# A 13-stage decoder on one core: TensorE multiplies constants into an unread bank behind the scores that run ahead

## The reference, cut to what matters

```
scores = q @ k.T (/ sqrt(8), + mask)          # 256 x 256
p      = softmax(scores, axis=-1)
out    = p @ v                                # 256 x 8
```

## Time and profile before

| | us |
|---|---|
| median of 3 timed runs | 1590.61 |
| profiled execution, own time | 1582.52 |
| its span (first to last instruction) | 1580.7 |
| TensorE busy | 1209.8 (77%) |
| TensorE weight loads | 607.2 (38%) |
| VectorE busy | 984.1 (62%) |
| ScalarE busy | 881.5 (56%) |
| GpSimd busy | 543.8 (34%) |

### The profile page before, as it was taken

One profiled execution on the slowest core, in us unless ns is written; L12 is line 12 of the kernel. 1 busy time (PEld: TensorE's weight loads), 2 busy tenths in 40 slices (PEclk: granted clock), 3 DMA queues, 4 the chain that ended last, 5 costly groups with the idle time before them and its releaser, 6 DMA issues. The chain is left out here.

```text
span 1580.7 us, 21176 instructions
## 1 busy us (share of the span) xinstructions
PE 1209.8 (77%) x6990; PEld 607.2 (38%) x6990; DVE 984.1 (62%) x1994; ACT 881.5 (56%) x1817; POOL 543.8 (34%) x673
## 2 busy tenths in 40 slices
PE   8999647266666677987657995977968988979886
PEld 3675422022222233542213552433444434734562
DVE  3673455999999927632757735446546658727752
ACT  3674144599999926874124871234634745724643
POOL 1462014488888843200224212011101223503440
PEclk9999887599999987998877997987986999999998
DMA  3000000000000015101006200015114110000000
GB/s 149 2 2 1 22 9 0 0 0 0 1 0 0 0 73 141 22 34 40 0 3 196 50 2 18 0 33 124 16 56 125 37 56 1 2 1 1 1 2 13
DMA packets 44108, 48.75 MB, mean 31 GB/s; under 512 B 3808, under 2 KB 40800, under 8 KB 42848
## 3 DMA queue, kind: packets, MB, share of 16 engines
q1 hardware_dynamic: 40688, 45.83, 10.0%
q10 hardware_dynamic: 3312, 1.57, 0.3%
HBM read 34.28 MB, written 13.11 MB: 30 GB/s over the span
## 5 line engine op out<-in xcount | busy, mean ns | idle before, releaser
L1548 POOL TENSOR_TENSOR L_attn_z<-L_attn_state,L_attn_r 128x1024 f32<-128x1024 f32 x64 | 151.0, 2360 | 21.6 <-DVE L_attn_state L1534 14.7
L1534 DVE TENSOR_TENSOR_SCAN L_attn_state<-bank,L_attn_w 128x512 f32<-128x512 f32 x128 | 148.9, 1205 | 0.0
L1445 PE MATMUL bank<-L_attn_z,const 128*128 128x512 f32 x256 | 139.4, 673 | 0.2 <-POOL L_attn_z L1552 0.2
L950 DVE CUSTOM_DVE_ANT_0 L_xattn_core_logits<-bank,L_xattn_mask 128x256 f32<-128x256 f32 x256 | 98.6, 422 | 45.1 <-PE bank L722 32.6
L1429 PE MATMUL bank<-L_attn_rows,L_attn_select 128*128 128x512 bf16 x96 | 36.2, 435 | 79.5 <-ACT L_attn_C L1497 42.9
L1485 ACT ACTIVATE L_attn_r<-L_attn_after_dt,L_attn_half_guard,L_attn_A 128x512 f32<-128x512 f32 x128 | 96.5, 802 | 0.0
L1475 ACT ACTIVATE bank<-L_attn_dt,L_attn_A 128x510 f32<-128x510 f32 x128 | 86.5, 676 | 12.8 <-DVE L_attn_state L1534 12.8
L862 ACT ACTIVATE L_xattn_core_probs<-bank 128x512 f32<-128x512 f32 x132 | 71.6, 596 | 35.6 <-PE bank L765 24.5
L1552 POOL TENSOR_TENSOR L_attn_z<-L_attn_z,L_attn_C 128x1024 f32<-128x1024 f32 x32 | 75.8, 2368 | 23.4 <-ACT L_attn_C L1497 23.3
L1515 DVE TENSOR_TENSOR L_attn_w<-bank,L_attn_udt 128x1024 f32<-128x1024 f32 x64 | 78.2, 1221 | 5.3 <-PE bank L1429 1.6
L722 PE MATMUL bank<-L_xattn_core_rows 48*128 48x256 bf16 x384 | 61.3, 302 | 17.2 <-DVE L_xattn_core_top L950 11.9
(11 more groups left out here) (500 smaller groups left out, 3042.9 us busy)
## 6 DMA issues: line engine op xcount, KB each, us to landing
L_xattn_core_rows<-L_xattn_core_slots SPq DMA_DIRECT2D x48, 96.0 KB, 2.3
L_xattn_core_rows<-L_xattn_core_slots SPq DMA_DIRECT2D x12, 384.0 KB, 6.1
weights<-in_pack_L_ffn SPq DMA_DIRECT2D x2, 2118.5 KB, 8.1
L_xattn_core_slots<-L_xattn_core_k_parts SPq DMA_DIRECT2D x24, 128.0 KB, 2.1
weights<-in_pack_L_ffn SPq DMA_DIRECT2D x1, 2824.0 KB, 12.3
L_xattn_core_slots<-L_xattn_core_q_parts SPq DMA_DIRECT2D x9, 192.0 KB, 2.2
weights<-in_pack_L_xattn SPq DMA_DIRECT2D x1, 1539.5 KB, 6.3
weights<-in_pack_L_attn SPq DMA_DIRECT2D x2, 768.0 KB, 9.4
```

Of the source, the lines that this page charges most:

```text
L950: last = nc.vector.tensor_tensor_reduce(logits[:, c], scores_bank[side][:, c * S:(c + 1) * S], mask[:, 2 * b + c, :], 1.0, MASKED, ALU.add ...
L1445: last = nc.tensor.matmul(y_bank[2 * c + half][:], ident, z[:, g % NS, c], start=False, stop=False, skip_group_check=True)
L1534: nc.vector.tensor_tensor_scan(state[:, g % NS, c, ::step], a_bank[c][:, ::step], w[:, g % 2, c, ::step], 0.0, ALU.mult, ALU.add).then_inc ...
L1548: nc.gpsimd.tensor_tensor(z[:, g % NS], state[:, g % NS], r[:, g % NS], ALU.mult).then_inc(z_done, 1)
```

## The change

In TensorE's loop of `attention8`, behind the scores of each pair with p below 0 (six of them), fp32 multiplications of the identity with the first 256 columns of x are put in, one without a mask and two with one. They write into the first half of bank 7. No semaphore is waited for or signalled by them.

```diff
             for p in range(-LEAD, NP + 3):
                 if p + LEAD < NP:
                     scores(p + LEAD)
+                if p < 0:
+                    for _ in range(2 if masked else 1):
+                        nc.tensor.matmul(out_bank[:, 0:S], K.w("ident"), K.x[:, 0:S], start=True, stop=True)
                 if 0 <= p < NP:
                     shifted(p)
                 if p % 2 == 0 and 0 <= p // 2 + 1 < NQ:
                     turn_shifts(p // 2 + 1)
```

## The result

The changed kernel took 1583.43 us (median of 15 runs, 1578.72 to 1593.14) against 1588.64 us for the kernel before (15 runs): 5.2 us less, ratio 0.9966 with a 95% interval of 0.9951 to 0.9982, so faster by 0.18 to 0.49%. One of the fifteen executions before, at 1680.00 us, is a slow one and is not in the ratio. The forecast was 6.2 us less, 1584.4 us, with a range of 1580.0 to 1590.5.

The account below looks back on a forecast made before the run. TensorE was the busiest engine, its clock falling to half in sparse attention leads and slowing the pairs behind. Gains of 3.8 + 0 + 1.2 + 1.2 = 6.2 us off the 1590.61 median gave 1584.4 us, range 1580.0 to 1590.5.

Parts of the forecast that it names:

- Fillers hidden at full clock: In the four leads, VectorE's maxima cover the fillers, 0.46 us each at full clock, so they cost nothing.
- VectorE's wait of 1.85 us at pair 1: Sign in the masked attentions: VectorE's wait for TensorE there, 1.85 us before, would be gone.
- The clock is held through the lead: In all four attentions, fp32 fillers between the scores keep TensorE's clock at 1.00, so pairs from 0 start at full clock.
- rival 4: Leads: the clock is low while fillers run and scores come late; 4.8 us slower, 1595.4 us; chance 0.08.
- Narrow pairs 0 to 3 hold it: Behind L3_xattn's lead, denser 48-row work keeps the full clock the fillers gained, making its 3.8 us safe.
- rival 1: L3_xattn's narrow pairs lose the clock soon after p = 0; 3.2 us less in all, 1587.4 us; chance 0.22.
- L3_xattn 3.8 us: Last attention: gain 3.8 us; 5.5 at most by TensorE, 4.2 by VectorE's pace, 0.4 allowed for ScalarE.
- L3_attn 0: Gain 0 in L3_attn: time won earlier is lost waiting for the third batch element's rows, 4.07 us before.
- L1_xattn and L2_xattn 1.2 each: Masked attentions: pairs behind the lead run at full clock; 1.2 us less each, taken between 0 and 1.5.
- rival 2: Both masked attentions lose the clock idling ahead of turn_shifts(0), L3_xattn gains fully; 3.8 us less, 1586.8 us; chance 0.15.
- the bound of about 1.5 us: Masked attentions: VectorE's 1.85 us wait and its own 0.92 us steps limit the gain to about 1.5 us each.
- The sum: Whole kernel: 3.8 + 0 + 1.2 + 1.2 = 6.2 us less, 1584.4 us; chance 0.43.

Follow-up runs that it names:

- third profile: The changed kernel, not edited further, profiled a third time: whole execution 1580.0 us, L3_xattn 65.7 us.
- second profile: The changed kernel, not edited further, profiled a second time, on another chip than the third and fourth: whole execution 1588.8 us, L3_xattn 71.0 us.
- fourth profile: The changed kernel, not edited further, profiled a fourth time: whole execution 1579.1 us, L3_xattn 65.7 us.
- e7: Against e4, its bf16 fillers use all 128 rows instead of 48: 1587.47 us in a single execution, L3_xattn 65.5 us.
- e3: Against the changed kernel, two fillers behind each early pair in all four attentions: 1582.7 us, ratio 0.9964 to the kernel before.
- e4: Against the changed kernel, fp32 fillers replaced by 48-row bf16 ones, four for each: 1588.36 us, ratio 0.9993 to the kernel before.
- e6: Changed kernel with lead fillers redistributed, none in L3_attn's lead, but 8 in its wait for the third batch element: 1579.98 us, ratio 0.9930 to the kernel before.

## Why the prediction was right, point by point

- **Fillers hidden at full clock.** Right. The rest of the lead of L3_xattn takes 5.80 us as before, and in the third profile VectorE has no wait above 0.5 us in either masked lead before the turn. VectorE's wait of 1.85 us at pair 1 is gone in L1_xattn (at most 0.55 us are left, in the second profile); in L2_xattn 1.31 us of it are left in three. The price: sixteen records in 3.72 us are 0.465 us a multiplication against the 0.46 of the sum; alone in the queue, one pair of records takes 0.70. At low clock a masked pair's two take about 2.0 us (609.95 to 611.96) where I had 1.62.
- **The clock is held through the lead.** Half right. The sign named for it, 1.00 in all four leads, is met in none of the four profiles. Of their sixteen leads seven lost the clock within 6 us of the first scores: two of L1_xattn, three of L3_attn, two of L3_xattn. One filler a pair is at the edge in the unmasked ones. The prediction had a low clock in the lead only as a single outcome for all attentions (rival 4), starting from a low clock at its start. It happens in single attentions, with a start at 1.00.
- **Narrow pairs 0 to 3 hold it (rival 1 against the forecast).** Right in L3_xattn: 1.00 from 1209.9 to 1216.3 in the third profile with nothing but 48-row work and the small turns on TensorE, and so in all seven profiles, experiments included, in which its lead had held. Not in L3_attn, for which the prediction did not ask: in the fourth profile and in e7 its lead held too, and the clock fell 12.2 us behind the first scores, in a wait of 1.75 and 2.58 us for the rows of the second batch element. In e3, where this wait was 0.27 us, it stayed. The rule of the Trainium skill ("TensorE: Matmul & The Clock Gate", "Why this matters for your kernels": keep TensorE continuously busy) gives the same for L3_xattn, but e4 disagrees with it as far as a rise goes: 5.84 of 6.00 us busy at 0.51, then 9.37 of 9.40 at 0.50.
- **L3_xattn 3.8 us.** 3.6 where held, against 5.5 by TensorE alone; VectorE's pace is what stands between, as the sum had it. That pace was read wrongly: two reductions of 682 ns are 1.36 us a pair, not the 1.2 taken from one short interval. The 0.4 us allowed for ScalarE happened to cover most of it, which is luck. values(0) comes 2.7 us sooner, not 3 to 4; the other 0.9 are the values themselves (1.07 us instead of 1.93). Where lost, 1.6 us more than before (rival 4 had 2.4).
- **L3_attn 0.** Right: 77.8 to 79.1 us with fillers, 77.3 to 78.9 without. The longer wait is plain in e3 (6.88 us); with the change, whose fillers held this lead in one profile of four, it was 3.5 to 4.6 us against 4.07 before. e6 shows the missing half of the argument: what that attention pays is not its lead but the low clock behind the wait, 3.5 us or so, which the prediction named and did not see as a place for a filler.
- **L1_xattn and L2_xattn 1.2 each.** The sum of 2.4 was about 2: L1_xattn 1.2 to 1.8 less; L2_xattn 2.1 less in one profile of four, and between 0.3 less and 0.4 more in the others. That is rival 2's mechanism in one of the two places: the idle time ahead of the turn (1.61 us, predicted 1.8) lost the clock in three of four profiles of L2_xattn. Held, both gain more than the bound of about 1.5 us. In L1_xattn a low clock inside the lead (0.72 in 607.2 to 611.5) cost little (89.7 us against 89.4 in the third profile, where it was held): VectorE waits 1.39 and 0.85 us for TensorE, but the turn, ahead of which TensorE waits 1.50 us for GpSimd in the third profile, starts only 0.3 us later, 11.0 instead of 10.7 us behind the first scores.
- **The sum.** If 2 of the 15 timed executions lost L3_xattn, as their mean clocks suggest, it is 3.6 x 13/15 - 1.6 x 2/15 = 2.9 us, L1_xattn 1.5, L2_xattn about 0.5: an estimate of 4.9 us, measured 5.2 to 5.4 (2.9 to 7.8 by the interval). With the share of the profiles, 2 of 4, it would be 3.0, which the interval allows as well, so how often the clock is lost stays open. The forecast of 6.2 was too high by L2_xattn's 0.7 and by the lost executions; that it came so near owes something to L1_xattn's 0.3 more.

## What to carry to other kernels

When TensorE's granted clock is low in the stretch behind a sparse one, fill the sparse stretch with multiplications of full height into a bank that is written afresh anyway; those of 48 rows did nothing here, however busy they kept the engine. The best places are waits that end by themselves (a DMA, another engine's long work), where the filler is free and the work behind it is paid at once, while in front of such a wait a faster engine only waits longer. A filler that just about holds the clock makes single executions differ by 5 us, so profile several and compare stages, not spans.

## What the runs showed of the hardware

- The same instructions at the same clock can hold it in one execution and lose it in the next (L3_xattn at 65.7 and 70.9 us, one kernel), with 0.6 to 0.7 us of idle time ahead of them in both losing profiles. The same 1.61 us of idle time in L2_xattn lost it in three profiles and not in the fourth.
- Among the scores of a lead, bf16 fillers of 128 rows kept TensorE at 1.00 (L2_xattn, 2.65 us busy of the first 3.40), those of 48 rows didn't (2.87 of 3.40 busy, then 0.50). Yet 48-row work that follows a held stretch ran on at 1.00 in L3_xattn (5.92 of 6.40 us busy), and lost it in L3_attn where a wait of 1.75 us stood in it. Before, the same work behind a lost lead was busy 9.07 of 9.10 us and got no faster.
- An fp32 multiplication of 128x256 costs 0.465 us at full clock, as two records of about 0.23 us each.
